# Relational values gathered in one run beside the score and segment loops, and read back in slot order in the last loop

## The reference

```python
for r in range(WQ.shape[0]):                       # 5 edge types
    Qn, Kn, Vn = nf @ WQ[r], nf @ WK[r], nf @ WV[r]
    e = Qn[tgt] @ a_q + Kn[src] @ a_k
    e = jnp.where(e >= 0, e, 0.2 * e)
    e_m = jnp.where(edge_type == r, e, -1e30)
    e_max = segment_max(e_m, tgt)
    e_exp = jnp.exp(e_m - e_max[tgt])
    e_sum = segment_sum(e_exp, tgt)
    attn = e_exp / (e_sum[tgt] + 1e-10)
    h = h + segment_sum(jnp.where((edge_type == r)[:, None], Vn[src] * attn[:, None], 0.0), tgt)
return elu(h)
```

## Time and profile before

| what | us |
|---|---|
| median of 3 runs | 6560.58 |
| the runs | 6554.14 to 6580.65 |
| the profiled execution in all | 6499.4 |
| its span, first to last instruction | 6497.7 |
| TensorE busy | 3728.7 (57%) |
| GpSimd busy | 3273.6 (50%) |
| VectorE busy | 2938.5 (45%) |
| ScalarE busy | 822.6 (13%) |

### The profile page before, as it was taken

How to read it: one execution, slowest core, us unless ns; L and a number is a source line. 1 busy time by engine, 2 the same in 40 slices (tenths; PEclk the granted TensorE clock), 3 DMA queues, 4 the chain that set the end, 5 groups by cost and what they waited for, 6 DMA issues and landing times. The chain is left out here.

```text
span 6497.7 us, 81708 instructions
## 1 busy us (share of the span) xinstructions
PE 3728.7 (57%) x19254; PEld 3244.4 (50%) x19255; DVE 2938.5 (45%) x9185; ACT 822.6 (13%) x1860; POOL 3273.6 (50%) x3327
## 2 busy tenths in 40 slices
PE   0000889866666466653644443677775666546665
PEld 0000788855655355542624332466665566346664
DVE  5000666643433333333794434266673444343334
ACT  0000111120111011120100000111111111311112
POOL 4775555536664466603004663166665566036662
PEclk9999777765555555565555555855555666768887
DMA  5232444432222222223402222211111111111112
GB/s 187 74 77 76 118 113 113 116 61 62 66 64 51 60 64 65 64 48 102 112 3 56 68 67 34 73 41 40 41 35 39 41 42 42 11 43 52 53 52 34
DMA packets 394236, 415.69 MB, mean 64 GB/s; under 512 B 230871, under 2 KB 296473, under 8 KB 394137
## 3 DMA queue, kind: packets, MB, share of 16 engines
q0 software_dynamic: 105984, 211.53, 13.1%
q1 hardware_dynamic: 233240, 141.69, 7.8%
q10 hardware_dynamic: 54912, 61.36, 3.5%
HBM read 325.69 MB, written 88.62 MB: 64 GB/s over the span
## 5 line engine op out<-in xcount | busy, mean ns | idle before, releaser
L603 POOL DMA_INDIRECT ring<-table_gine,idx x1248 | 1220.5, 978 | 962.0 <-DVE mraw L641 407.8
L1518 PE MATMUL ps<-msg,oh 128*128 128x128 f32 (+2 forms) x4160 | 919.0, 389 | 476.8 <-DVE HA L641 425.2
L1518 PEld LDWEIGHTS ps<-msg,oh 128*128 128x128 f32 x4160 | 819.6, 289 | 544.4 <-DVE HA L641 419.9
L641 DVE TENSOR_TENSOR mraw<-ps,ring 128x512 f32<-128x512 f32 x520 | 358.4, 689 | 1076.2 <-remote 671.7
L641 DVE TENSOR_TENSOR HA<-HA,ps 128x128 f32 (+2 forms) x2080 | 598.3, 288 | 249.3 <-DVE HA L641 124.9
L622 POOL DMA_INDIRECT ring<-table_rel,idx x368 | 350.9, 954 | 628.4 <-PE ps L1663 458.7
L603 POOL DMA_INDIRECT ring<-table_keys,idx x416 | 459.2, 1104 | 406.2 <-SPq L184 202.4
L1527 PE MATMUL ps<-wt,ear 64*128 64x128 f32 x2496 | 599.4, 410 | 60.9 <-DMA ear<-edge_attr_T 44.0
L603 POOL DMA_INDIRECT ring<-table_msg,idx x416 | 399.7, 961 | 464.4 <-SPq L184 215.9
L1527 PEld LDWEIGHTS ps<-wt,ear 64*128 64x128 f32 x2496 | 511.9, 300 | 130.0 <-issue 120.3
L603 POOL DMA_INDIRECT ring<-table_values,idx x416 | 400.3, 962 | 293.5 <-DVE msg L641 135.6
(11 more groups left out here) (288 smaller groups left out, 6103.1 us busy)
## 6 DMA issues: line engine op xcount, KB each, us to landing
ear<-edge_attr_T SPq DMA_DIRECT2D x312, 128.0 KB
oh<-slot_rows ACTq DMA_DIRECT2D x104, 256.0 KB
slot_records<-msg SPq DMA_DIRECT2D x32, 650.0 KB, 11.2
arena<-slot_records SPq DMA_DIRECT2D x104, 200.0 KB
edge_attr_T<-arena ACTq DMA_DIRECT2D x104, 192.0 KB
ring<-table_gine,idx POOLq DMA_INDIRECT x1248
ear<-slot_rows ACTq DMA_DIRECT2D x104, 128.0 KB
arena<-in_edge_attr SPq DMA_DIRECT2D x50, 250.0 KB
```

Of the source, the lines that this page charges most:

```text
L603: pool.indirect_dma_start(out=ring[:, k % 4, j, 0:width], out_offset=None, in_=table[:, :], in_offset=bass.IndirectOffsetOnAxis(ap=idx[:, ...
L641: return V.tensor_tensor(o, x, y, op)
L1518: ins = M.matmul(out_of(t, j), oh[:, t.s4, j, :], x, start=True, stop=True)
```

## The change

GpSimd gathers all 416 tiles in one run, beginning where the first gather stood. They go to `vdeep`, twelve slots in the same space as `vpre`. Four batches back must have landed before a batch is issued, and from the thirteenth on the slot's last write-out must have landed. SyncE waits for each batch and writes it to `vals` ("slot_values"), in slot order, 256 KB each. In the last loop ScalarE gets a third stage, `values_back`, with lag 2: one transfer per batch from `vals` into `ring`, after the write-out and, from the fifth batch on, after the sums of the batch four back. `att_sums` waits for this transfer and always reads `ring`. Its unrolled part goes from 20 turns to 12.

```diff
-PRE = 12
+DEEP = 12
@@ SyncE, behind the table's writes @@
+            for k in range(NB):
+                sp.wait_ge(qa.gath[k % 4], 16 * B * (k // 4 + 1))
+                if k >= 4:
+                    sp.wait_ge(values_out[k % 4], 16 * (k // 4))
+                sp.dma_start(vals[k], vdeep[:, k % DEEP].rearrange("p j d -> p (j d)")).then_inc(values_out[k % 4], 16)
@@ GpSimd @@
             for k in range(NB):
-                if k >= PRE + 4:
-                    pool.wait_ge(qa["sums"], k - 3)
+                if k >= 4:
+                    pool.wait_ge(qa.gath[k % 4], 16 * B * (k // 4))
+                if k >= DEEP:
+                    pool.wait_ge(values_out[k % 4], 16 * ((k - DEEP) // 4 + 1))
                 for j in range(B):
-                    row = bass.IndirectOffsetOnAxis(ap=idx5[:, k * B + j:k * B + j + 1], axis=0)
-                    if k < PRE:
-                        pool.indirect_dma_start(out=vpre[:, k, j, :], out_offset=None, in_=tab1[:, :],
-                                                in_offset=row).then_inc(first_values, 16)
-                    else:
-                        pool.indirect_dma_start(out=ring[:, k % 4, j, 0:D], out_offset=None, in_=tab1[:, :],
-                                                in_offset=row).then_inc(qa.gath[k % 4], 16)
+                    pool.indirect_dma_start(
+                        out=vdeep[:, k % DEEP, j, :], out_offset=None, in_=tab1[:, :],
+                        in_offset=bass.IndirectOffsetOnAxis(ap=idx5[:, k * B + j:k * B + j + 1], axis=0)).then_inc(qa.gath[k % 4], 16)
@@ ScalarE, last loop @@
+            def values_back(t):
+                act.wait_ge(values_out[t.s4], t.u * 16 + 16)
+                if t.late(4):
+                    act.wait_ge(qa["sums"], t.n - 3)
+                act.dma_start(ring[:, t.s4, :, 0:D], vals[bass.ds(t.k, 1)].rearrange("a p (j d) -> p (a j) d", j=B)).then_inc(values_in[t.s4], 16)
-            run(act, [(4, att_exp), (0, att_in)])
+            run(act, [(4, att_exp), (0, att_in), (2, values_back)])
@@ TensorE, att_sums @@
-                early = isinstance(t.k, int) and t.k < PRE
-                if early:
-                    pe.wait_ge(first_values, 16 * B * PRE)
-                else:
-                    pe.wait_ge(qa.gath[t.s4], t.u * (16 * B) + (16 * B - 16 * B * (PRE // 4)))
+                pe.wait_ge(values_in[t.s4], t.u * 16 + 16)
...
-            run(pe, [(6, att_sums), (2, att_lookups)], lead=PRE // 4 + 2)
+            run(pe, [(6, att_sums), (2, att_lookups)])
```

More of the change, by code:

```diff
@@ L75, in build @@
         slotrow = dram("slot_rows", [2, NT, P], BF16)
+        vals = dram("slot_values", [NB, P, B * D])
         tab2k = dram("table_keys", [NPAD * NREL, D])
@@ L157, in build @@
         rowsd_out = sem("slot_rows_out")
-        first_values = sem("first_values_in")
+        values_in = [sem(f"slot_values_in{h}") for h in range(4)]
+        values_out = [sem(f"slot_values_out{h}") for h in range(4)]
         drin = [sem(f"dst_rows_in{h}") for h in range(4)]
@@ L251, in late, with run @@
                 return not isinstance(self.n, int) or self.n >= lag
-        def run(eng, stages, of=0, lead=0):
+        def run(eng, stages, of=0):
             deep = max(lag for lag, _ in stages)
-            lead = max(lead, -(-deep // 4) + 1)
+            lead = -(-deep // 4) + 1
             def turn(r, s):
@@ L360, in build @@
         rest = aren[:, 15600:15600 + 2 * NCODE]
-        vpre = HA[:, 0:PRE * B * D].rearrange("p (k j d) -> p k j d", k=PRE, j=B)
+        vdeep = HA[:, 0:DEEP * B * D].rearrange("p (k j d) -> p k j d", k=DEEP, j=B)
         FR = aren[0:GT, 9360:9360 + 513]
@@ L1663, in att_sums @@
                     ins = M.matmul(psf[:, bass.ds(blocks[j] * D, D)], oh[:, t.s4, j, :],
-                                   vpre[:, t.k, j, :] if early else ring[:, t.s4, j, 0:D], start=False, stop=False)
+                                   ring[:, t.s4, j, 0:D], start=False, stop=False)
                 ins.then_inc(qa["sums"], 1)
-            run(pe, [(6, att_sums), (2, att_lookups)], lead=PRE // 4 + 2)
+            run(pe, [(6, att_sums), (2, att_lookups)])
             for z in range(7):
```

## The result

The changed kernel is slower here: 6794.19 us median (6793.20 to 6812.12, 4 runs) against 6562.81 us before (6554.14 to 6580.65), ratio 1.0355 (95%: 1.0328 to 1.0383). The forecast was 6730 us, slower; the time lies within the range.

A forecast was written before the change was run, and what follows sets the result against it. Gathers were taken to hold the last loop, and unbroken gather runs to delay TensorE's signals in the lookup loop. +403 - 233 = +170 us on 6499.4, plus 61 carried, gave 6730 us; range 6570 to 6850.

The forecast's parts named there:

- The last loop: Final loop of the relational stage, freed of gathers: 109 turns at 3.03 us, 330 us against 563.5, 233 us saved.
- Rival 4: Last loop: waiting for the read-back keeps every turn as long as now, nothing saved, +403, 6963 us; chance 0.05.
- The gathers' length: GpSimd's one run from 2943.8 us: 416 gathers at 1.248 us, 519 us, ending at 3463.
- the steps on these waits: GpSimd's run: waits for landed batches and written-out slots are met long before, make no pause, priced at nothing.
- The turns beside them: Lookup loop beside the gathers: one turn per 25 us, 18 turns by 3470 us, saving 37 us later.
- The silence after the run: Lookup loop: after the last gather, 6.4 us more before TensorE's reader goes on, as in the earlier trace.
- the lookup term: Lookup loop held up beside the gathers: its rest and the segment work end 440 - 37 = 403 us later.
- The carried difference: Whole kernel: the median lies 61 us above the profiled execution's 6499.4 us; carried unchanged into the forecast.
- "Remote" waits of 350 us: Sign in the lookup loop: ScalarE's and VectorE's waits marked "remote" together some 350 us instead of 80.
- Rival 3: Lookup loop: nothing holds the lookups after the first 80 us, no shift, 6560 - 233 = 6328 us; chance 0.17.
- The point at which the change turns good: Lookup loop: gain once the shift is under 233 us, 102 turns in 440 us, one per 4.3 us.

The follow-up runs named there:

- Q: Four chips on which the kernel before took 5682 to 5709 us, no wait marked "remote"; the changed kernel took 5570.07 us against 5683.77, ratio 0.9801.
- P: One chip on which the kernel before took 6496 us, near the record's 6563, with "remote" waits; the changed kernel as it stands never ran there.
- the fills: Changed kernel with every gather replaced by three GpSimd fills of SBUF, no transfer started; 5536.9 us beside 5693.2 for the kernel before.
- plain transfers: Changed kernel with each of the 416 gathers replaced by a plain 64 KB transfer of 128 neighbouring rows; 6237.0 us against 6495.9 for the kernel before.

## Why the prediction was right, and where it was off

**Right in direction and mechanism for the chip of the record.** That the sign of the change hangs on the chip was not foreseen: on Q it would have been wrong. On the record the lookup loop stood nearly still until the gathers had ended, the segment work followed unchanged, and the last loop was freed. Step by step:

- *The last loop*, -233 forecast, -232.5 measured. 109 turns at 3.03 us gave 330 us, measured are 331.0; the transfer that reads a batch back lands in 3.1 us (median), and no turn waits for it. Rival 4 is out.
- *The gathers' length*, 519 us forecast, 557 measured, +38. The first 160 stand 1.25 us apart, as in the earlier trace rows; from there to the end it is 1.40. The longest lasted 1.95 us, and no wait for a landing or a written slot is named, so the steps on these waits hold. On P it is the same (1.25, then 1.40 from the same place), and on Q nearly (1.28, then 1.40), so it does not go with the late signals. Its cause was not looked for.
- *The turns beside them*, one per 25 us forecast, one per 44.9 measured. Forecast were 23 copies by 3470, measured are 15 by 3525.6. The taken value was the wrong one of three gaps (9.2, 30.9, 43.4 us). These were not a scatter but a growth: by the order of turns, the copies at 2955.84, 2986.72 and 3030.12 in the earlier trace rows are of turns whose matmuls had ended 8, 37 and 71 us before. I had set the last copy against the matmuls just before it (2990.2), which are those of the next turn. Read rightly, the lateness grows from turn to turn, and the last gap is the least that should be carried on; that the growth ends at 86 us only the trace of after shows. At 44 us a turn the term is some 420 us instead of 403.
- *The silence after the run*, 6.4 us forecast, 26.8 measured. That, too, goes with signals already 86 us late when the gathers end.
- Together the lookup term was +403 forecast and +474 measured: 38 for the longer run, 20 for the silence behind it, 13 for the turns not done by then; 71 in sum.
- *The carried difference.* The profiled execution of before was 61 us quicker than its median, and I carried that unchanged. The trace of after shows where 52 of it lie: 26.7 us ahead of the first gather (2970.5 against 2943.8) and 25.3 behind the last sum (2532.7 against 2507.4), outside of all that the change touches. So the 294 us between the two spans (6791.5 - 6497.7) are 242 of the stage and 52 of this; between the medians it is 231, where I had forecast 170. The 6499.4 us of the profiled execution is none of the four timed runs of before (6554 us at least), but the level of P.

The term of the sum that was mis-sized is thus the lookup loop, by 71 us. It is all of the 64 us by which 6794 lies above 6730; the carried difference, 61 us forecast and 52 found, takes some of it back.

**Where the signs agreed only by half.** "Remote" waits of 350 us on ScalarE and VectorE in the loop were named as a sign, instead of 80 (which is one engine's number: 78.8 and 82.8 before); the trace gives them 222 and 214 us, and 363 and 347 us more as "issue". By the silences, not by the label, the sign held.

**Not foreseen.** Rival 3, signals not held at all, had 0.17 and a time of 6328. On the chips where it is so the change does win, but half of what rival 3 said: 114 us, not 233. It took the last loop of the record (563 us) for a loop bound by gathers alone. On Q, where nothing is late, that loop takes 495 us before the change, so 68 us of it go with the late signals as well. And the freed loop takes 356 us and not 331, as 110 gathers and their writes still run beside it (without a gather, with the fills, it took 336). The point at which the change turns good was put at one lookup turn per 4.3 us; on either side of it nothing was measured nearer than 2.7 us (plain transfers on P, -259 us) and 44.9 us.

The section of the Trainium skill weighed in the prediction, "SBUF — State Buffer", "Who interferes with whom", says that a DMA doesn't contend with a compute engine. The plain transfers agree for P: a DMA share of 0.92 and not one late signal, at 2.7 against 2.0 us a turn. The indirect ones on P are not explained by it, nor by its second rule, on VectorE and GpSimd: ScalarE stands as still as VectorE.

**What is shown and what is open.** Shown: on P, by one run each, late signals in the lookup loop come with GpSimd's indirect transfers, not with bytes, SyncE's writes or TensorE's register load; on Q they don't come at all; where they come, they cost the lookup loop 463 us, all of this change's loss. Not shown: what in an indirect transfer does it (a GpSimd busy in another way was only tried on Q), whether the signal leaves TensorE late or reaches its readers late, why 86 us, why only on some chips, and whether pieces or another place for the run would keep the gain where signals are late.

## What to carry to other kernels

Before an engine's long stream is moved beside a loop, look at a stretch where the two already meet, and number the turns on both sides: a copy belongs to the matmuls of its own turn, not to the last ones before it. If lateness grows from turn to turn, calculate with its last value at the least. And a wait that the profile can't name, above all in many stages of one trace, may belong to the chip: such a kernel should be measured on several before a change that trades one kind of wait for another is taken or dropped; this one is 3.6% slower on one kind and 2.0% faster on the other.

## What the runs showed of the hardware

- The same kernel, before, takes 6496 to 6563 us on some chips and 5682 to 5709 us on others, at granted clocks of 0.65 and 0.70 over the span. The long time goes with waits marked "remote" (some 2640 and 2770 us in sum), the short with none. Whether it is the chip or a state of it was not separated.
- Where they occur, a signal of TensorE comes up to 86 us after its matmuls beside an unbroken run of indirect gathers, while VectorE's one-hot that ends at 3527.30 is followed by TensorE's matmul at 3528.03, 0.7 us later. A turn takes 44.8 to 44.9 us there, whether the gathers stand 1.25 or 1.40 us apart.
- 416 plain transfers of 64 KB started by GpSimd take 236 us, 0.57 us each, at a DMA share of 0.98 in that stretch; as many indirect ones take 557 to 562 us.
